# Column maxima of an attention score matrix: VectorE transposes and maximises each score bank in one instruction, TensorE makes one small transpose per head, and the finished rows travel by DMA on ScalarE's queue

## The reference

```python
attn = einsum('bhid,bhjd->bhij', q * scale, k)
attn = attn + take_along_axis(qL, idx)                  # bias by distance, from the query
attn = attn + swapaxes(take_along_axis(kL, idx), 2, 3)  # bias by distance, from the key
attn = softmax(attn, axis=-1)                           # needs the maximum over keys j, per query i
out  = einsum('bhij,bhjd->bhid', attn, v) + (sums of attn by distance) @ rpe_v_table
```

## Time and profile before

| | |
|---|---|
| Time, three runs | median 1713.56 us (1693.01 to 1720.0) |
| Profiled execution | 1715.73 us, of which the span is 1713.9 us |
| Granted TensorE clock, mean over the span | 0.912 |
| Busy: PE, PEld, DVE, ACT, POOL | 85%, 58%, 62%, 54%, 26% of the span |
| DMA | 335.02 MB, mean 195 GB/s |

### The profile page before, as it was taken

The page is one execution under the profiler, slowest core; times in us unless marked ns, Lnnn a source line. Parts: engine busy times, 40 slices in busy tenths (PEclk is TensorE's granted clock), DMA queues, the critical chain, the costliest instruction groups (busy, mean ns, idle before and its releaser), DMA issues.

```text
span 1713.9 us, 76370 instructions
## 1 busy us (share of the span) xinstructions
PE 1451.0 (85%) x33658; PEld 1000.1 (58%) x33658; DVE 1061.0 (62%) x2333; ACT 920.5 (54%) x1600; POOL 439.2 (26%) x424
## 2 busy tenths in 40 slices
PE   3783688888888888799989888999998888899987
PEld 2441355555556566566658656666666655666666
DVE  6683577676667766766654456666655555666662
ACT  2242265556556555466651356666666555666664
POOL 3452111111011110111234123333333223333331
PEclk9896598899899989999995699999999999999999
DMA  3545466666566656666765467778767767777863
GB/s 85 159 146 152 146 209 211 198 212 209 189 199 204 195 180 196 191 212 214 239 209 155 127 195 229 235 222 247 235 207 214 207 186 213 214 221 220 234 177 125
DMA packets 232917, 335.02 MB, mean 195 GB/s; under 512 B 29937, under 2 KB 151018, under 8 KB 232587
## 3 DMA queue, kind: packets, MB, share of 16 engines
q1 hardware_dynamic: 221114, 323.30, 60.6%
q0 software_dynamic: 11472, 6.83, 2.9%
HBM read 169.52 MB, written 112.89 MB: 165 GB/s over the span
## 4 chain that ended last, share of the span: by engine, by line
PE 58%; DVE 19%; issue 11%; ACT 7%; DMA 2%; SPq 2%; POOL 0%; another core or an unknown queue 0%; ACTq 0%; DVEq 0%; POOLq 0%
PE PS L667 48%; DVE accm L1374 5%; PE PS L912 4%; PE PS L881 4%; DVE mx L1382 4%; ACT Qs L1088 3%; DVE dq_s L1411 2%; ACT PT L1062 2%; SPq L410 1%; DVE KT L1312 1%; ACT dq_e L1092 1%; PE PS L900 1%; DMA dq_s<-dq_d 1%; DVE mparts L1385 1%; DVE mparts L1387 1%
## 5 line engine op out<-in xcount | busy, mean ns | idle before, releaser
L667 PE MATMUL PS<-Qs,Ks 79*32 79x512 bf16 (+31 forms) x11904 | 709.7, 328 | 98.8 <-DVE accm L1374 55.0
L1062 ACT ACTIVATE PT<-PS 128x512 f32<-128x512 f32 x1024 | 584.8, 598 | 374.8 <-PE PS L667 369.0
L1374 DVE TENSOR_TENSOR accm<-PS,accm 128x512 f32<-128x512 f32 x896 | 593.6, 686 | 300.2 <-PE PS L667 283.8
L667 PEld LDWEIGHTS PS<-Qs,Ks 79*32 79x32 bf16 (+1 forms) x11904 | 334.4, 99 | 302.2 <-DVE accm L1374 73.4
L667 PE MATMUL PS<-PT,Vst 128*9 128x256 f32 (+7 forms) x7552 | 348.7, 290 | 5.6 <-issue 5.0
L626 POOL CAST ajp<-dq_s 128x508 bf16<-128x508 f32 x128 | 78.3, 612 | 926.4 <-DVE dq_s L1411 925.2
L667 PE MATMUL PS<-WT,eye 96*32 96x96 bf16 (+2 forms) x4352 | 308.7, 210 | 4.1 <-issue 4.1
L667 PEld LDWEIGHTS PS<-PT,Vst 128*9 128x9 f32 x7552 | 188.1, 92 | 72.1 <-issue 27.0
L667 PEld LDWEIGHTS PS<-WT,eye 96*32 96x32 bf16 x4352 | 191.8, 100 | 26.3 <-issue 10.0
L1382 DVE TENSOR_REDUCE mx<-PS 128x8 f32<-128x1024 f32 x64 | 78.4, 1225 | 130.6 <-PE PS L881 123.5
L628 POOL TENSOR_TENSOR ajp<-dq_s,ajp 128x508 bf16<-128x508 f32 x128 | 150.2, 1173 | 10.4
(11 more groups left out here) (204 smaller groups left out, 1260.1 us busy)
## 6 DMA issues: line engine op xcount, KB each, us to landing
aj_d<-ajp SPq DMA_DIRECT2D x64, 768.0 KB
WT<-aj_d SPq DMA_DIRECT2D x192, 256.0 KB
WP<-PT SPq DMA_DIRECT2D x128, 384.0 KB, 3.6
TOE<-toe_d SPq DMA_DIRECT2D x64, 768.0 KB
dq_d<-dq_e SPq DMA_DIRECT2D x64, 512.0 KB
dq_s<-dq_d SPq DMA_DIRECT2D x64, 512.0 KB, 5.5
q_stack<-PT SPq DMA_DIRECT2D x24, 256.0 KB, 2.5
Qs<-q_stack SPq DMA_DIRECT2D x64, 96.0 KB
```

Of the source, the lines that this page charges most:

```text
L667: return pe.matmul(o, l, r, start=start, stop=stop, skip_group_check=True)
L1062: act.activation(PT[:, TILE + N * J + 512 * half:TILE + N * J + 512 * half + 512], PS[:, 2 + u % 2, :], ACT.Exp).then_inc(s2_read, 1)
L1374: dve.tensor_tensor(dst, PS[:, s % 2, :], dst, ALU.max).then_inc(s1_read, 1)
```

## The change

- **Pass 1's banks.** ScalarE copies none. VectorE reads each of the 16 banks with one `tensor_reduce` with `apply_transpose=True`: the 128 x 512 bank is seen as 32 x 32 blocks, each transposed, and the maximum taken over the 32 keys of a block. 128 x 16 numbers result, kept in `tops`.
- **Per head.** At slot 0 VectorE reduces `tops` over the 8 key tiles to `top` (128 x 32). At slot 1 TensorE makes one transpose of it to 32 x 128, and VectorE takes the maximum over the 4 partition groups with a negated result, and cuts it in two casts, two subtractions and a last cast of 32 x 32 numbers.
- **The rows.** The 8 matmuls and ScalarE's copy are gone. At slot 3 ScalarE's queue issues three DMAs, from 32 partitions x 64 bytes into one row of `Qs` each, and pass 2 waits for their landing (`mrow_in`).
- **LAG** is 6 instead of 4: pass 2, and the values behind it, run two slots later against pass 1. What other units in `MISC` wait for is `top_read` (VectorE has read the small transpose) in place of `mrow_ready`.
- `accm` is gone; buffers of the first and last phases that lay in it (`XT`, `QF`, `CT`) lie in `PT` and `WT`.

The diff, cut to its core:

```diff
-LAG = 4
+LAG = 6
...
 # TensorE
-                if which == 1 and u == 0:
-                    pe.wait_ge(mrow_ready, h + 1)
+                if which == 1 and u == 0:
+                    pe.wait_ge(mrow_in, 48 * (h + 1))
...
-                    if s == 3 and on(0):
-                        pe.wait_ge(mparts_ready, h + 1)
-                        for I_ in range(NJ):
-                            ins = mm(MISC[0:3, I_ * P:(I_ + 1) * P], mparts[:, I_, :], identb[:, :], start=I_ % 4 == 0)
-                        ins.then_inc(mrow_psum, 1)
-                    if s == 0 and on(0):
-                        pe.wait_ge(s1_read, SLOTS * h + SLOTS)
+                    if s == 1 and on(0):
+                        pe.wait_ge(top_ready, h + 1)
                         misc_free(h, (dq_copied, h + 4))
-                        for I_ in range(NJ):
-                            ins = pe.transpose(MISC[:, I_ * P:(I_ + 1) * P], accm[:, c % 2, I_ * P:(I_ + 1) * P], ident[:, :])
-                        ins.then_inc(accT_psum, 1)
+                        pe.transpose(PS[0:TILE, 6, 0:P], top[:, :], ident[:, :]).then_inc(top_psum, 1)
...
 # ScalarE
-                    if s < 2 and on(1):
-                        act.wait_ge(s1_ready, SLOTS * (h + 1) + s + 1)
...
-                        act.activation(accm[:, (c + 1) % 2, 512 * s:512 * s + 512], PS[:, s, :], ACT.Copy).then_inc(s1_read, 1)
                     if s == 3 and on(0):
-                        act.wait_ge(mrow_psum, h + 1)
-                        act.wait_ge(s1_ready, SLOTS * h + SLOTS)
-                        act.activation(Qs[ROW_M:ROW_M + 3, h % RING, :], MISC[0:3, :], ACT.Copy).then_inc(mrow_ready, 1)
+                        act.wait_ge(mparts_ready, h + 1)
+                        for n in range(3):
+                            act.dma_start(Qs[ROW_M + n:ROW_M + n + 1, h % RING, :].rearrange("p (c j) -> p c j", j=TILE),
+                                          mparts[:, n, :]).then_inc(mrow_in, 16)
...
 # VectorE
+                    if s == 0 and on(0):
+                        dve.wait_ge(s1_read, SLOTS * h + SLOTS)
+                        wait(dve, top_psum, h)
+                        dve.tensor_reduce(top[:, :], tops[:, h % 2, :, :].rearrange("p j c -> p c j"), AX.X, ALU.max).then_inc(top_ready, 1)
-                    if on(1) and s >= 2:
+                    if on(1):
                         dve.wait_ge(s1_ready, SLOTS * (h + 1) + s + 1)
-                        dst = accm[:, (c + 1) % 2, 512 * (s % 2):512 * (s % 2) + 512]
-                        dve.wait_ge(s1_read, SLOTS * (h + 1) + max(2, s - 1))
-                        dve.tensor_tensor(dst, PS[:, s % 2, :], dst, ALU.max).then_inc(s1_read, 1)
-                    if s == 0 and on(0):
-                        dve.wait_ge(accT_psum, h + 1)
+                        dve.tensor_reduce(tops[:, (h + 1) % 2, s // 2, 16 * (s % 2):16 * (s % 2) + 16],
+                                          PS[:, s % 2, :].rearrange("p (c i) -> p c i", i=TILE), AX.X, ALU.max,
+                                          apply_transpose=True).then_inc(s1_read, 1)
+                    if s == 1 and on(0):
...
-                        hstep(dve.tensor_reduce(mx[:, 0, :], MISC.rearrange("p (a b) -> p a b", a=NJ), AX.X, ALU.max), 1)
-                        wait(dve, mrow_psum, h)
-                        hstep(dve.tensor_scalar(mx[:, 1, :], mx[:, 0, :], -1.0, None, ALU.mult), 2)
...
+                        dve.wait_ge(top_psum, h + 1)
+                        wait(dve, mrow_in, 48 * h)
+                        dve.tensor_reduce(mx[:, 0, :], PS[0:TILE, 6, 0:P].rearrange("p (g j) -> p j g", g=4), AX.X, ALU.max,
+                                          negate=True).then_inc(top_read, 1)
+                        dve.wait_ge(top_read, h + 1)
+                        hstep(dve.tensor_copy(mparts[:, 0, :], mx[:, 0, :]), 1)
+                        hstep(dve.tensor_tensor(mx[:, 1, :], mx[:, 0, :], mparts[:, 0, :], ALU.subtract), 2)
+                        hstep(dve.tensor_copy(mparts[:, 1, :], mx[:, 1, :]), 3)
+                        hstep(dve.tensor_tensor(mx[:, 2, :], mx[:, 1, :], mparts[:, 1, :], ALU.subtract), 4)
+                        dve.tensor_copy(mparts[:, 2, :], mx[:, 2, :]).then_inc(mparts_ready, 1)
```

More of the change, by code:

```diff
@@ L131, in program @@
         PT = sb("PT", [P, TILE + NJ * N + TILE])
-        accm = sb("accm", [P, 2, N])
+        tops = sb("tops", [P, 2, NJ, TILE])
+        top = sb("top", [P, TILE])
         Qs = sb("Qs", [ROWS, RING, N], BF16)
@@ L147, in program @@
         Oev = sb("Oev", [P, 2, 256])
[L148 to L149 removed]
+        mx = sb("mx", [TILE, 3, TILE])
+        mparts = sb("mparts", [TILE, 3, TILE], BF16)
         rden = sb("rden", [P, 4, 2])
@@ L185, in program @@
         RV66, at = cut(ew, 0, [P, QB, E + 2])
-        accf = accm[:, :, :].rearrange("p a b -> p (a b)")
         WPf = WP[:, :, :].rearrange("p a b -> p (a b)")
         TOEf = TOE[:, :, :].rearrange("p a b -> p (a b)")
-        XT, at = cut(accf, 0, [P, 2, 512])
-        QF, at = cut(accf, at, [P, 512])
         CF, fz = cut(PT, 0, [P, 512])
@@ L207, in program @@
         Z, fz = cut(PT, fz, [P, 1024])
+        XT, fz = cut(PT, fz, [P, 2, 512])
+        QF, fz = cut(PT, fz, [P, 512])
         assert fz <= TILE + NJ * N
         WTf = WT[:, :, :].rearrange("p a b -> p (a b)")
+        CT = WTf[:, 2 * N:3 * N].rearrange("p (a n) -> p a n", a=2)
         WTb = WTf.bitcast(BF16).rearrange("p (r s j n) -> p r s j n", r=3, s=4, j=NJ)
@@ L293, in program @@
             sem("s1_ready"), sem("s1_read"), sem("s2_ready"), sem("s2_read"))
-        accT_psum, mparts_ready, mrow_psum, mrow_ready = (
-            sem("accT_psum"), sem("mparts_ready"), sem("mrow_psum"), sem("mrow_ready"))
+        top_ready, top_psum, top_read, mparts_ready, mrow_in = (
+            sem("top_ready"), sem("top_psum"), sem("top_read"), sem("mparts_ready"), sem("mrow_in"))
         dq_psum, dq_copied, dq_out, dq_in = sem("dq_psum"), sem("dq_copied"), sem("dq_out"), sem("dq_in")
@@ L1234, in _ @@
             dve.wait_ge(tabs_in, 48)
-            step(dve.tensor_copy(mx[:, 0, 0:2], tres[:, :, LOW]))
-            step(dve.tensor_tensor(tres[:, :, :], tres[:, :, :], mx[:, 0, 0:2].unsqueeze(2).broadcast_to([P, 2, P]), ALU.subtract))
+            step(dve.tensor_copy(top[:, 0:2], tres[:, :, LOW]))
+            step(dve.tensor_tensor(tres[:, :, :], tres[:, :, :], top[:, 0:2].unsqueeze(2).broadcast_to([P, 2, P]), ALU.subtract))
             step(dve.tensor_scalar(tres[:, 1, :], tres[:, 1, :], SC, None, ALU.mult))
@@ L1382, in iteration @@
-                        hstep(dve.tensor_reduce(mx[:, 0, :], MISC.rearrange("p (a b) -> p a b", a=NJ), AX.X, ALU.max), 1)
-                        wait(dve, mrow_psum, h)
-                        hstep(dve.tensor_scalar(mx[:, 1, :], mx[:, 0, :], -1.0, None, ALU.mult), 2)
-                        hstep(dve.tensor_copy(mparts[:, :, 0], mx[:, 1, :]), 3)
-                        hstep(dve.tensor_tensor(mx[:, 2, :], mx[:, 1, :], mparts[:, :, 0], ALU.subtract), 4)
-                        hstep(dve.tensor_copy(mparts[:, :, 1], mx[:, 2, :]), 5)
@@ L1388, in iteration @@
-                        hstep(dve.tensor_tensor(mx[:, 3, :], mx[:, 2, :], mparts[:, :, 1], ALU.subtract), 6)
-                        dve.tensor_copy(mparts[:, :, 2], mx[:, 3, :]).then_inc(mparts_ready, 1)
+                            dve.wait_ge(max_step, 4 * h + m)
+                        dve.wait_ge(top_psum, h + 1)
+                        wait(dve, mrow_in, 48 * h)
+                        dve.tensor_reduce(mx[:, 0, :], PS[0:TILE, 6, 0:P].rearrange("p (g j) -> p j g", g=4), AX.X, ALU.max,
+                                          negate=True).then_inc(top_read, 1)
```

18 lines of the change are left out of this document (6 added, 12 removed).

## The result

| | before | after |
|---|---|---|
| Median, four runs each | 1703.95 us | 1788.67 us (1773.97 to 1796.31) |
| Ratio, 95% interval | 1 | 1.051 (1.038 to 1.064) |
| Profiled execution; span | 1715.73; 1713.9 us | 1773.97; 1772.2 us |
| Granted TensorE clock | 0.912 | 0.859 |

What follows compares the result with a forecast made beforehand. PE, 85% busy, was taken as the engine to relieve, with the DRAM loop limiting the gain. Gains of 43, 17, 22 and 9 us less 1 for the tail took 1715.7 to 1626, predicted as 1625 us; own range 1590 to 1665.

Steps and rivals of the forecast that it cites:

- The step that failed: ScalarE's queue, slot 3: three DMA issues take 1.0 us, replacing an equal delay of the row copy; net 0.
- LAG.: Loads tied to pass 2 move two slots later, needed several us later: 0; the tail's extra slots cost 1.2 us once.
- rival (c): Loop through DRAM gets longer, 1 us more on each leg, as moved loads and row DMAs share engines: 1725 us, chance 0.15.
- The DRAM loop: Store and load back of `dq`, awaited by PE in slot 5, end together with PE's own work, limiting the gain.
- the sum: Gains per stretch of heads, limited by room in front of line 912: 90 us off 1715.7, giving 1626 us.
- 2.2 of PE's path: PE's path per head: 2.66 us of old maxima work removed, less the new transpose and waits, leaves 2.2 us.
- the stalls called issue: PE gaps the profile does not explain: around 35 us in sum; whether they meet the new order left untold.
- The transposing reduction: VectorE's new read of each pass 1 bank: 720 ns, within bounds of 686 and 1225 ns.
- rival (a): The transposing reduction takes 1225 ns and makes VectorE the bound: 1890 us, chance 0.13.
- (d): Rows come late, or one reduction takes 0.8 to 0.9 us; PE waits about 1.5 us in slot 6: 1680 us, chance 0.12.
- VectorE's wait: In slots 6 to 10 VectorE holds PE up; five reductions there, 34 ns longer each, cost 0.2 us per head.
- PE idle before the transposes of `dq_s`: Sign in slot 5 of the fast heads: PE waits there 0.5 to 2 us each.

Runs made afterwards that it cites:

- spreading: Changed kernel with ScalarE's three row DMA issues placed one each in slots 3, 4 and 5, an exponential between them: 1731.28 us, 1.004 of the kernel before.
- transfers are light: Kernels with 1.7 of 4.3 MB of transfers per head left out, output wrong: kernel before 1670.74 us; with LAG 6, 1685.42 us.
- SyncE version: Changed kernel with its three row DMAs issued by SyncE instead of ScalarE: 1733.08 us, 1.003 of the kernel before.
- light SyncE version: SyncE version with 1.7 of 4.3 MB of transfers per head left out, output wrong: 1596.88 us, 0.932 of the kernel before.

## Why the prediction was wrong

**The step that failed** is ScalarE's: "so 1.0 us for three at the low end, 0 if ScalarE only hands over; I take 1.0 ... the delay replaces an equal one of L1088. Net on the path: 0". The three take 1.80 us (1.83 in the median head), not 1.0, so some 0.8 us more than the 1.01 of the copy that they replace, and what stands behind them is the exponential of slot 3, for whose bank PE waits: 54.7 us in 49 heads. I had named the queue behind the issues and dismissed it by ScalarE's mean of 54%; but PE waits in a slot, not in a mean, and its time at the lower clock grew with these waits (427 us, 354 once they are spread). Taken out, by SyncE or by spreading, the time falls by 4.5%; put into before, it rises by 3.8%.

**The second** is "**LAG.** ... several us later, so 0". `WT` was indeed in time, but LAG = 6 costs the kernel before 2.8%, and 0.7% where the transfers are light: so most of it comes of the loads that moved. That they now lie beside the loop's store, and beside `near` and its fetches, is argued from the waits that grew. I had this as rival (c), at 0.15 and 1725 us, and without the block the change comes to 1733 us. That is near by luck: (c) lengthens both legs of the loop by 1 us, while store to load grew by 0.6 us in the SyncE version, the landing not at all (5.6 us), and "issue" grew by 50 us; nor did it include the block.

**The DRAM loop** held in part. In the SyncE version PE comes to it first in 26 heads, where the sum had the room in front of it as the limit in 48. The size of the gain did not hold: the sum has -5.2%, the maxima gave -2.4% against before with LAG 6, and -4.9% where the transfers are light (some 1.3 us per head of the 2.2 of PE's path; both values include the waits behind the row copy). Another term that was mis-sized is what I put down as "the stalls called issue lie around 35 us in sum": they were 45 us in before from 195 to 1650 us and became 65 to 95.

**What held.** The transposing reduction: 720 ns forecast, 698 measured; rival (a) is out, and of (d) neither half came. The reduction of 256 elements takes 602 ns, not 0.42 us, that of 128 takes 241 (0.28 forecast), the small transpose 303 ns (0.27). The rows land in 2.3 us in the SyncE version (2.2 forecast); PE waited for them once in the changed kernel, 1.5 us. VectorE's wait grew from 51.5 to 65.8 us, 0.2 us a head, as forecast, though with light transfers it grew by 0.5. VectorE's busy time grew by 0.8 us per head, not 1.2. So the terms of the exchange itself were right to some 0.4 us a head, and the two terms put at nothing decided the sign.

The signs that I named: the reduction at 0.69 to 0.75 us came true; "PE idle before the transposes of `dq_s`" came true in the SyncE version only, since in the changed kernel PE came late itself; heads of 21.3 us in the first stretch became 25.2.

**Open.** No version with all its transfers beat the kernel before by more than its interval. Whether one DMA for all three rows would do, and whether `near` in another slot would meet its fetches elsewhere, was not tried. Why the light SyncE version waits 30 us more for VectorE's reading of the banks than before does is not settled beyond VectorE's having more to do per head; and the part of "issue" that each transfer causes was not separated.

## What to carry to other kernels

A DMA issue is an instruction of the engine whose queue it is on: price it by its own row (mostly 0.5 to 0.6 us here), and place issues one by one between that engine's other work, never several ahead of the instruction that the busiest engine waits for. A pipeline made deeper to hide a new transfer moves every load tied to it; follow those too, and try the depth alone first. Where the bottleneck engine's clock falls after its waits, a wait of 0.8 us can cost more than its length. And add up what the busiest engine waits for over all lines of a change: one line that grew (83.6 against 53.2 us) can stand beside another that is gone (38.0).

## What the runs showed of the hardware

- **A single DMA issue runs beside an activation, three in a row hold ScalarE back.** The issues themselves cost nearly the same: 1.83 us for three in a row, 0.51, 0.57 and 0.51 us when one stands in each slot (medians over the heads). But ScalarE computes beside 9 of 127 us of them in the first case and beside 89 of 116 in the second. The Trainium skill ("DMA: Bandwidth & Descriptors", section Issuing engines are not separate DMA queues) calls the time to initiate a DMA "usually small relative to the DMA itself"; for these rows it is 0.6 us each beside 2.3 us to the landing.
- **A transposing reduction of a 128 x 512 bank costs what a plain elementwise maximum of it does**, 698 against 686 ns; the strided reduction of 256 elements, 602 ns, costs 2.35 ns per element, the most of the four reductions here (1.36 for the transposing one).
- **PE's gaps called "issue" go with the instruction queue and with bulk traffic.** Gaps of up to 3.4 us in the changed kernel and 4.7 in the SyncE version end 1.2 to 1.6 us after 16 KB packets of that queue. They shrink by 44% (before) and 63% (SyncE version) when 1.7 MB of a head's transfers are left out, but by 11% and 2% when 768 KB of them (TOE) are.
- **The clock loses more than the wait.** 3 us at 0.50 after 1.0 us of idle between 1209 and 1212 us; over the changed kernel 427 us at the lower level against 229, which lengthened PE's unchanged work by some 100 us, while its idle time rose by 54 us only. The two don't go together in every version: with `dq_d`'s store first, the kernel before idles for 287 us instead of 263 and has 183 us at the lower level.
